# A decoder layer on one core: one norm chain in self-attention, value weights one step sooner, another VectorE order at the end of cross-attention

## The reference, cut to what matters

```python
x = x + attn(_layernorm(x))      # self-attention
x = x + xattn(_layernorm(x), ctx, ctx, mask)   # cross-attention to 128 keys, 16 heads of 64
x = x + ffn(_layernorm(x))       # shared expert and 32 routed experts, top 1

def attn(residual):              # _layernorm once more, with gain g and bias b
    x = _layernorm(residual, g, b)
    q = heads of x (4 of 128);  k = w_fc.reshape(-1, 128);  v = w_proj.T.reshape(-1, 128)
    return residual + square(relu(q k^T)) v
```

## Time and profile before

| | us |
|---|---|
| median of 3 runs | 2863.79 (2860.95 to 2864.35) |
| the profiled execution, its own time | 2861.03 |
| its span in the trace | 2859.4 |
| TensorE busy in the span | 2772.2 (97%) |
| VectorE busy | 1804.1 (63%) |
| ScalarE busy | 1592.0 (56%) |
| GpSimd busy | 1015.1 (36%) |
| granted TensorE clock, mean | 0.996 of full speed |

### The profile page before, as it was taken

One profiled execution on the slowest core, in us unless ns is written; L12 is line 12 of the kernel. 1 busy time (PEld: TensorE's weight loads), 2 busy tenths in 40 slices (PEclk: granted clock), 3 DMA queues, 4 the chain that ended last, 5 costly groups with the idle time before them and its releaser, 6 DMA issues.

```text
span 2859.4 us, 46307 instructions
## 1 busy us (share of the span) xinstructions
PE 2772.2 (97%) x13287; PEld 2284.7 (80%) x13289; DVE 1804.1 (63%) x2744; ACT 1592.0 (56%) x2744; POOL 1015.1 (36%) x692
## 2 busy tenths in 40 slices
PE   7999999999989999999899999999999999999998
PEld 5888888888778887788778888887788888888886
DVE  6566666666776665667563433435885855676776
ACT  6888888887665554566431111112574744565665
POOL 6888888887522221222200000000232322232332
PEclk9999999999999999999999999999999999999999
DMA  1000000002221102110221111112986964786884
GB/s 63 26 27 11 26 26 26 17 24 70 75 67 45 44 29 59 34 37 28 96 89 59 61 66 60 59 66 87 344 314 216 355 214 146 271 296 228 291 289 175
DMA packets 190791, 322.70 MB, mean 113 GB/s; under 512 B 23528, under 2 KB 49128, under 8 KB 190720
## 3 DMA queue, kind: packets, MB, share of 16 engines
q1 hardware_dynamic: 179440, 296.61, 30.2%
q0 software_dynamic: 11280, 25.20, 2.6%
HBM read 286.86 MB, written 46.66 MB: 117 GB/s over the span
## 4 chain that ended last, share of the span: by engine, by line
PE 86%; DVE 6%; ACT 4%; issue 2%; POOL 1%; ACTq 0%; DMA 0%; DVEq 0%; POOLq 0%
PE d_pG L1977 9%; PE d_pU L1977 8%; PE a_pS L47 4%; PE a_pS L49 4%; PE a_pS L48 4%; PE a_pO L47 4%; PE a_pO L49 4%; PE a_pO L48 4%; PE d_pD L47 3%; PE d_pD L49 3%; PE d_pD L48 3%; PE c_pD L47 2%; PE c_pD L49 2%; PE c_pG L47 2%; PE c_pD L48 2%
## 5 line engine op out<-in xcount | busy, mean ns | idle before, releaser
L157 POOL TENSOR_TENSOR a_pL<-a_p,a_pH 128x1024 fp32r<-128x1024 f32 x256 | 617.8, 2418 | 163.7 <-DVE a_p L348 161.7
L1215 DVE TENSOR_TENSOR e_wL<-e_raw,e_wH 128x1024 fp32r<-128x1024 f32 x384 | 450.3, 1217 | 36.1 <-PE d_pU L1977 24.4
L348 DVE TENSOR_TENSOR a_p<-a_r,a_pS 128x1024 f32<-128x1024 f32 x256 | 312.2, 1220 | 243.4 <-ACT a_r L165 236.2
L1210 ACT CAST e_wH<-e_raw 128x1024 fp32r<-128x1024 f32 x384 | 384.5, 1053 | 86.3 <-PE d_pD L49 59.3
L670 POOL TENSOR_TENSOR b_S<-b_S,b_ri 128x512 f32<-128x512 f32 x128 | 133.2, 1041 | 501.0 <-DVE b_ri L831 501.0
L165 ACT ACTIVATE a_r<-a_pS 128x1024 f32<-128x1024 f32 x256 | 261.8, 1023 | 80.3 <-PE a_pS L49 78.6
L165 ACT ACTIVATE a_pH<-a_r 128x1024 fp32r<-128x1024 f32 x256 | 271.9, 1062 | 9.1
L687 ACT ACTIVATE b_S<-b_S,b_nm 128x128 f32<-128x128 f32 x512 | 198.8, 393 | 35.3 <-DVE b_nm L826 34.7
L1459 POOL DMA_INDIRECT out<-d_og,c_iw x46 | 86.5, 1880 | 359.2 <-DVE d_og L1851 359.2
L47 PE MATMUL a_pS<-a_qH,a_kH 128*128 (+1 forms) x512 | 205.0, 400 | 1.3 <-DVE a_p L348 1.2
L47 PE MATMUL a_pO<-a_pH,a_vH 128*128 128x512 f32 x512 | 199.8, 390 | 1.5 <-POOL a_pL L157 1.5
(11 more groups left out here) (308 smaller groups left out, 7251.2 us busy)
## 6 DMA issues: line engine op xcount, KB each, us to landing
e_raw<-in_L_ffn_routed_gate_w SPq DMA_DIRECT2D x256, 256.0 KB, 4.5
e_raw<-in_L_ffn_routed_up_w SPq DMA_DIRECT2D x256, 256.0 KB, 5.7
e_raw<-in_L_ffn_routed_down_w SPq DMA_DIRECT2D x128, 512.0 KB, 6.8
a_xb<-in_x SPq DMA_DIRECT2D x8, 1024.0 KB, 5.5
x<-a_base SPq DMA_DIRECT2D x32, 256.0 KB, 2.3
b_xr<-x SPq DMA_DIRECT2D x32, 256.0 KB, 3.2
x<-b_xr SPq DMA_DIRECT2D x32, 256.0 KB, 3.0
c_xb<-x SPq DMA_DIRECT2D x32, 256.0 KB, 2.9
```

The costliest lines, as they stand in the source:

```text
L157: nc.gpsimd.tensor_tensor(pL[:, j % RING, :, :], p[:, j % 2, :, :], pH[:, j % RING, :, :].bitcast(F32), ALU.subtract).then_inc(s["low"], 1)
L348: v.tensor_tensor(p[:, j % 2, :, :], r[:, j % 2, :, :], pS[j % 2][:, :, :], ALU.mult).then_inc(s["p"], 1)
L1210: copy(self.wH[n][:, :, :], self.raw[n][:, :, :]).then_inc(self.s["high"], 1)
L1215: unit.tensor_tensor(self.wL[n][:, :, :], self.raw[n][:, :, :], self.wH[n][:, :, :].bitcast(self.F32), self.sub).then_inc(self.s["low"], 1)
```

## The change

In the self-attention the two scales are made side by side: r1 from v + e and r1 r2 from v (1 + e) + e^2, as two halves of 128 x 2 x 4 tiles, in 5 parts with 14 links in place of 9 with 29. At the start the first head's 128 columns of the four tiles are normalised and handed to TensorE by a semaphore of their own, and the other 384 columns after the first copy a_qH. Value weights (1, n) are copied in the steps 12, 14, 16 and 18 (their subtraction follows one step later). In the last two steps of cross-attention VectorE takes the subtractions of pieces 0 and 1 in step 7, after the maximum, and t_low there ahead of the mask; pieces 2 and 3 go into `ending`. A semaphore that nothing waits for (warm) is dropped.

```diff
-    LINKS = 29
+    LINKS = 14
...
         def normalize(G, t):
             if t == 0:
                 act.wait_ge(s["own"], LINKS * (G + 1))
-                if not (isinstance(G, int) and G == 0):
-                    act.wait_ge(s["xt"], NH * G)
+                act.wait_ge(s["xt"], NH * G)
             scaled(qn[:, t, :], G, t, scale, shift).then_inc(s["normed"], 1)
+
+        def normalize_first(t, columns, count):
+            scaled(qn[:, t, columns], 0, t, scale, shift, columns).then_inc(s[count], 1)
...
+        act.wait_ge(s["own"], LINKS)
         for t in range(GT):
-            normalize(0, t)
+            normalize_first(t, slice(0, P), "first")
         q_high(0, 0)
+        for t in range(GT):
+            normalize_first(t, slice(P, C), "normed")
...
+            for w in (w2, w2_ps):
+                v.tensor_scalar(w[:, 0, :], mv_ps[:, :, 1], EPS, None, ALU.add)
+                m = v.tensor_scalar(w[:, 1, :], mv_ps[:, :, 1], 1.0 + EPS, EPS * EPS, ALU.mult, ALU.add)
+            link(m)
...
+        def newton(link):
+            link(v.scalar_tensor_tensor(out=t2_ps, in0=y2_ps, scalar=-0.5, in1=y2[:, :, :], op0=ALU.mult, op1=ALU.mult))
+            link(v.tensor_tensor(t2_ps, t2_ps, w2[:, :, :], ALU.mult))
+            both(link, lambda out: v.scalar_tensor_tensor(out=out, in0=t2_ps, scalar=1.5, in1=y2[:, :, :], op0=ALU.add, op1=ALU.mult))
+
+        def row_scales(link):
+            v.tensor_scalar(up[:, :], y2_ps[:, 0, :], 1.0, None, ALU.add)
+            v.tensor_scalar(scale[:, :], y2_ps[:, 1, :], 1.0, None, ALU.mult)
+            for out, y in ((off, y2[:, 0, :]), (shift, y2[:, 1, :])):
+                m = v.scalar_tensor_tensor(out=out[:, :], in0=mv_ps[:, :, 0], scalar=-1.0, in1=y, op0=ALU.mult, op1=ALU.mult)
+            link(m)
...
-        PARTS = 9
+        PARTS = 5
...
             if h == 0:
-                pe.wait_ge(s["normed"], GT * G + GT)
+                first = isinstance(G, int) and G == 0
+                pe.wait_ge(s["first"], GT) if first else pe.wait_ge(s["normed"], GT * G + GT)
+            if isinstance(G, int) and G == 0 and h == 1:
+                pe.wait_ge(s["normed"], GT)
...
-    W_HIGH_AT = {1: (0, 0), 4: (0, 1), 7: (0, 2), 10: (0, 3), 13: (1, 0), 15: (1, 1), 17: (1, 2), 19: (1, 3),
+    W_HIGH_AT = {1: (0, 0), 4: (0, 1), 7: (0, 2), 10: (0, 3), 12: (1, 0), 14: (1, 1), 16: (1, 2), 18: (1, 3),
...
-                soon = b > pb and j == 0 or j == NPAIR - 2 and not last
+                soon = b > pb and j == 0 or j == NPAIR - 2 or j == NPAIR - 1 and last
...
                 maximum(n, j)
-                if j != NPAIR - 2 and not (last and j == NPAIR - 1):
+                if last and j == NPAIR - 1:
+                    aside(j)
+                elif j != NPAIR - 2:
                     q_low(n + 2, (j + 2) % NPAIR)
...
-                if j in (1, 6, 7) and last:
+                if j == 1 and last:
                     aside(j)
...
             else:
-                w_low(2 * (j - 6))
-                w_low(2 * (j - 6) + 1)
+                w_low(0)
+                w_low(1)
...
             x_low(0, 0)
+            w_low(2)
             norm(0, 3)
+            w_low(3)
             out_stats(g, 0)
```

More of the change, by code:

```diff
@@ L79, in self_attention @@
     st = at(small, "st", [P, GT, 6], F32)
-    var, var1, var2, r1, r2, up, off, scale, shift, gT, bT = (at(small + 96 + 32 * i, n, [P, GT], F32) for i, n in
-                                                              enumerate("v v1 v2 r1 r2 up off scale shift gT bT".split()))
+    w2, y2 = (at(small + 96 + 32 * i, n, [P, 2, GT], F32) for i, n in enumerate(("w2", "y2")))
+    up, off, scale, shift, gT, bT = (at(small + 160 + 32 * i, n, [P, GT], F32) for i, n in
+                                     enumerate("up off scale shift gT bT".split()))
     names = ExitStack()
@@ L168, in piece, with scaled @@
             return a.rearrange("p (a c) -> p a c", a=KC)
-        def scaled(out, G, t, scale, shift):
-            return nc.scalar.activation(out, xb[:, bass.ds(G % 2, 1), t, :].rearrange("p o c -> p (o c)"), ACT.Identity,
-                                        bias=shift[:, t:t + 1], scale=scale[:, t:t + 1])
+        def scaled(out, G, t, scale, shift, columns=slice(0, C)):
+            rows = xb[:, bass.ds(G % 2, 1), t, columns].rearrange("p o c -> p (o c)")
+            return nc.scalar.activation(out, rows, ACT.Identity, bias=shift[:, t:t + 1], scale=scale[:, t:t + 1])
         def normalize(G, t):
@@ L249, in aggregate @@
             link(m)
-            v.tensor_scalar(var[:, :], mv_ps[:, :, 1], 1.0, None, ALU.mult)
-            v.tensor_scalar(var1[:, :], mv_ps[:, :, 1], EPS, None, ALU.add)
-            link(v.tensor_scalar(var_ps, mv_ps[:, :, 1], EPS, None, ALU.add))
-        def both(link, ps, own, op):
-            op(ps)
-            link(op(own))
-        def seed(link, y_ps, y):
-            link(v.tensor_single_scalar(tmp_ps.bitcast(I32), var_ps.bitcast(I32), 1, op=ALU.logical_shift_right))
-            both(link, y_ps, y[:, :], lambda out: v.tensor_scalar(out.bitcast(I32), tmp_ps.bitcast(I32), -1.0, float(0x5F3759DF),
-                                                                  ALU.mult, ALU.add))
@@ L264, in newton @@
-        def newton(link, y_ps, y, var):
-            link(v.scalar_tensor_tensor(out=tmp_ps, in0=y_ps, scalar=-0.5, in1=y[:, :], op0=ALU.mult, op1=ALU.mult))
-            link(v.tensor_tensor(tmp_ps, tmp_ps, var[:, :], ALU.mult))
-            both(link, y_ps, y[:, :], lambda out: v.scalar_tensor_tensor(out=out, in0=tmp_ps, scalar=1.5, in1=y[:, :], op0=ALU.add, op1=ALU.mult))
-        def second_variance(link):
-            link(v.tensor_tensor(tmp_ps, r1_ps, r1[:, :], ALU.mult))
-            link(v.tensor_tensor(tmp_ps, tmp_ps, var[:, :], ALU.mult))
-            both(link, var_ps, var2[:, :], lambda out: v.tensor_scalar(out, tmp_ps, EPS, None, ALU.add))
@@ new lines, in aggregate, with both, seed @@
+            link(m)
+        def both(link, op):
+            op(y2_ps)
+            link(op(y2[:, :, :]))
+        def seed(link):
+            link(v.tensor_single_scalar(t2_ps.bitcast(I32), w2_ps.bitcast(I32), 1, op=ALU.logical_shift_right))
+            both(link, lambda out: v.tensor_scalar(out.bitcast(I32), t2_ps.bitcast(I32), -1.0, float(0x5F3759DF), ALU.mult, ALU.add))
+        def newton(link):
+            link(v.scalar_tensor_tensor(out=t2_ps, in0=y2_ps, scalar=-0.5, in1=y2[:, :, :], op0=ALU.mult, op1=ALU.mult))
+            link(v.tensor_tensor(t2_ps, t2_ps, w2[:, :, :], ALU.mult))
+            both(link, lambda out: v.scalar_tensor_tensor(out=out, in0=t2_ps, scalar=1.5, in1=y2[:, :, :], op0=ALU.add, op1=ALU.mult))
@@ L283, in scales @@
                 aggregate(G, link)
-                seed(link, r1_ps, r1)
+                seed(link)
             elif part <= 3:
-                newton(link, r1_ps, r1, var1)
-            elif part == 4:
-                second_variance(link)
-                seed(link, r2_ps, r2)
-            elif part <= 7:
-                newton(link, r2_ps, r2, var2)
-            else:
-                residual_scales(link)
-        PARTS = 9
+                newton(link)
+            else:
+                row_scales(link)
+        PARTS = 5
         def q_affine(G, h):
@@ L1310, in feed_forward @@
          ("const g_in rH rL x_in0 x_in1 r_in0 r_in1 normed xt xH xL gate up sig gated h hH hL logit_ps lt logit top own score xs xs_out"
[L1311 removed]
+          " down sum out0 out1 w_in0 w_in1 w_in2 w_in3 w_high w_low").split()}
     rs = {n: ctx.enter_context(nc.semaphore("r_" + n)) for n in
@@ L1521, in _ @@
         nc.scalar.activation(rH, rw[:, :, :], ACT.Copy).then_inc(s["rH"], 1)
-        nc.scalar.activation(first_silu[:, :], ident[0:1, 0:1], ACT.Sigmoid).then_inc(s["warm"], 1)
+        nc.scalar.activation(first_silu[:, :], ident[0:1, 0:1], ACT.Sigmoid)
         w_high(KC)
```

10 lines of the change are left out of this document (2 added, 8 removed).

## The result

The changed kernel takes 2839.52 us, the median of six runs (2837.18 to 2841.95). The kernel before, run beside it, takes 2863.81 us (six runs, 2860.80 to 2865.39). The ratio is 0.9917, with a 95% interval of 0.9904 to 0.9930: faster by 24.3 us. The forecast was 2843.0, with a range of 2837 to 2852.

What follows compares the result with a forecast made beforehand. TensorE, busy 97% of the span, was taken as the bound, so only its stands could be won. 3.4 + 5.7 + 10.8 = 19.9 us off 2861.0, adjusted towards the median, gave 2843 us, range 2837 to 2852.

Steps and rivals of the forecast that it cites:

- The start: Kernel start: shorter VectorE chain and split normalisation bring TensorE's first transposes 3.4 us earlier, bounds 1.9 and 3.9.
- The value weights: TensorE's two waits on b_wL: earlier copies gain 5.7 us, including 1.2 us for low clock; bounds 1.5 and 7.1.
- So 1.1 us of the second wait stays: Value weights: the last moved subtraction ends near 744.0 us, TensorE ready at 742.9, leaving 1.1 us of wait.
- My hand schedule: Value weights: hand-worked VectorE times after the move, a_p of steps 16, 18, 19 ending near 726.6, 735.9, 740.1 us.
- The rule weighed there: Value weights: VectorE instructions with two SBUF inputs and GpSimd ones reading SBUF exclude each other, whichever starts first.
- 15.1 us, the sum by that reading: Total gain if four moved subtractions each held GpSimd up 1.2 us and all 4.8 us reached TensorE.
- GpSimd keeps the value weights late: Rival, chance 0.12: moved subtractions find GpSimd busy, value weights gain only 1.5 us; sum 15.7, time 2847 us.
- The end: End of cross-attention: VectorE's new order removes both long waits on b_tL, last products 10.8 us earlier; bounds 8.5 and 11.5.
- the end gives the moved subtractions back: Rival, chance 0.09: `ending` loses 2.3 us to subtractions and as much to a late reload; gain 15.3, time 2848 us.
- the change doesn't do what it says: Rival, chance 0.03: other TensorE waits fill both long gaps, only the start's gain is won; 2860 us, no change.
- The sum: Whole kernel: gains of 3.4 at the start, 5.7 at the value weights and 10.8 at the end total 19.9 us.
- From the profiled execution's 2861.0 us: Step from gain to time: 2861.0 becomes 2841.1 us; adding the median's 2.8 us offset gives 2843.9, taken as 2843.

Runs made afterwards that it cites:

- after_again: The changed kernel itself, run again on another chip; median 2839.40 us, ratio 0.9920 to the kernel before.
- start_only: Kernel before with the self-attention part alone (one chain of 14 links, first 128 columns first); median 2858.86 us, ratio 0.9984.
- values_only: Kernel before with the value weights' copies in steps 12, 14, 16 and 18 alone; median 2854.20 us, ratio 0.9967.
- values_first_pair: Kernel before with value pieces (1,0) and (1,1) alone copied in steps 12 and 14; median 2859.21 us, ratio 0.9987.
- chain_only: Kernel before with the single chain alone, the four tiles normalised whole; median 2860.31 us, ratio 0.9990.
- end_only: Kernel before with VectorE's new order in cross-attention's last two steps and behind it alone; median 2851.83 us, ratio 0.9962.
- split_only: Kernel before with the first 128 columns normalised ahead of the rest, old chains kept; median 2862.43 us, ratio 0.9995.
- end_second_pair: Kernel before with only the subtractions of pieces 2 and 3 moved into `ending`; median 2858.43 us, ratio 0.9982.
- warm_gap: Changed kernel with eight identity transposes on TensorE after the key transposes; median 2838.15 us, ratio 0.9914 to the kernel before.
- values_filled: Kernel before with TensorE's two waits on b_wL filled with 20 and 14 identity transposes; median 2860.64 us, ratio 0.9991.
- warm_both: Changed kernel with 40 identity transposes ahead of the key transposes and 12 behind; median 2837.47 us, ratio 0.9912 to the kernel before.

## Why the prediction was right, and where it was off

**The start**: predicted 3.4 us, with bounds of 1.9 and 3.9. Measured 3.4 at the first scores, and 3.5 to 3.7 by b_k1H in two traces of three. The steps hold one by one: chain until 12.8 us (forecast 12.8), ScalarE late with a_kH (14.0 forecast, 13.95), pieces 1.64 us for 1.5, transposes at 15.53 for 15.5, the rest 2.49 us for 2.5. What was not in the sum is the clock of the first scores: at half clock in the first trace after, it took 1.3 us of the gain (27.8 against 26.4 us at the stand behind a_vL), and at full clock in after_again and start_only nothing.

**The value weights**: predicted 5.7 us, bounds 1.5 and 7.1; measured 6.8 and 6.9. This is the mis-sized term. The step that failed is "So 1.1 us of the second wait stays": none stayed. My hand schedule had the subtraction of (1, 3) end near 744.0 us with TensorE ready at 742.9. The trace to hold against it is that of values_only, whose start is before's (b_k1H at 696.4 us for 696.2). TensorE was there at 742.93, as forecast, but the subtraction ended at 742.66: a_p of the steps 16, 18 and 19 ended at 726.4, 735.1 and 739.1 us where I had 726.6, 735.9 and 740.1, so VectorE was earlier by 0.2, 0.8, 1.0 and at last 1.3 us. In the trace after all of this lies 2.4 us earlier (740.25 and 740.53), as its b_k1H does. The margin is 0.3 us in both. That subtractions beside GpSimd stretch was right in kind: 2.98 and 2.98 us, 1.78 at (1, 1).

The rule weighed there (the Trainium skill, SBUF — State Buffer, "Who interferes with whom") shows here in one direction: the instruction that starts second is blocked for what is left of the other. The subtraction at 728.59 us took 2.98 us, which is the rest of GpSimd's low part (until 730.49 us) and 1.1 of its own. The other direction, 1.2 us lost on GpSimd four times over, didn't occur: all eight low parts from 710 to 744 us take 2.39 to 2.41 us, and none starts while one of the subtractions runs, so no run here shows that direction. So 15.1 us, the sum by that reading, was too low. The rival *GpSimd keeps the value weights late* fell.

**The end**: predicted 10.8 us, bounds 8.5 and 11.5; measured 10.7 to 10.8 in all traces with this part. Remaining waits forecast at 1.9, 0.7 and 0.8 us are 1.95 (1404.53), 0.78 and 0.82 (1412.38); the fourth, 1.84 us for the last b_aL (1415.44), was there before as well. The moved subtractions cost nothing, as forecast: VectorE's idle 1.33 and 2.40 us in `ending` shrank to 0 and 1.53. The rival *the end gives the moved subtractions back* fell with it, and so did "the change doesn't do what it says".

**The sum**: 19.9 us against 19.1 and 21.6 in two traces. **The time**: 2843.0 against 2839.5. The medians differ by 24.3 us, 4.4 more than the sum. After_again, whose profiled execution lies at its median, has 1.7 of them in its ledger: 0.3 at the start, 1.2 at the value weights, 1.1 behind c_pG, less 0.1 at the end and 0.8 in cross-attention. The other 2.7 are in "From the profiled execution's 2861.0 us": I carried the offset of 2.8 us between it and the median over to the changed kernel, as if the change couldn't touch it. Two of three executions of before take about 3 us more than the profiled one. By the traces named above that is 1.8 us of half clock behind the second wait for the value weights, which goes with the wait, and about 1.0 us in cross-attention, which both traces of the changed kernel have too. Counted from such an execution, the value weights give 6.9 + 1.8 = 8.7 us, cross-attention 0.2, and with 3.7, 10.7 and 1.1 the ledger comes to 24.4 us, for 24.0 to 24.3 measured. This is an estimate, since no trace shows such an execution of before. By it the value weights are above their bound of 7.1: I had 1.2 us for the clock, behind the first wait alone. For values_only it makes 6.8 + 1.8 = 8.6 us against 9.9 by the medians, whose interval reaches from 6.0 to 12.9.

**Luck.** That 2839.5 lies in the range of 2837 to 2852 is owed in part to how the range was counted. The gain of 24.3 us (20.0 to 27.5 by the interval) is larger than all high ends together (22.5). From the median of 2863.8 us these give 2841.3, and the measured time is below that. It is inside because the lower end was counted from the profiled execution's 2861 and then widened by 1.5 us.

## What to carry to other kernels

When the value of an edit is a stand of TensorE, count the wait in the rows, and add the half clock that may follow it as a separate term with its own chance: a profile shows one draw of it. Where profiled execution and median differ by more than the spread of the runs around their mode, look for such a stand before forecasting from the profile. A wait that can't be shortened can be filled with throw-away transposes, which here recovered the clock's share alone. And when two traces of different kernels are subtracted, compare the clock window by window first, also where the change does nothing: values_first_pair's 3.0 us would else be taken for the worth of its pair.

## What the runs showed of the hardware that was not expected

The same stand, in the same kernel text, is followed by half clock in some executions and not in others. Behind the second wait for b_wL, 2.3 to 2.4 us, the clock was 1.00 in before, start_only and chain_only and 0.91 in end_only, split_only, end_second_pair and values_first_pair; of these the first three take 66.0 to 67.2 us from the first values product to b_pQ, where before takes 64.2. Behind the stand for a_vL (2.29 to 2.33 us in every kernel) it fell in five traces (after, warm_gap, split_only, end_second_pair and values_filled) and stayed up in the other eight. Behind the stand of 2.32 us for b_S it fell in seven and stayed up in six.

A window of the profile can read a clock of 1.00 where there is no record of the clock. In after:

```profile
17.60:22.00 4.40, 4.40 (x16) 3.59 (x15) 0.69 (x1) 3.07 (x6) 0.00 (x0) 1.00 0.00 0
```

The stretch reads 1.00 with sixteen passes, although the passes from 19.2 to 21.7 us lie 0.43 us apart; after_again, at a spacing of 0.23, fits 22 into the same window. The first record of the clock in after's trace starts at 21.6 us, at full clock, which is where the spacing changes. In chain_only it starts at 13.1 us, and there the half clock of 18 to 20 us is recorded (0.52). Near the start of a trace the spacing is what to go by.

Identity transposes count for the clock. The sixteen key transposes behind forty of the same kind in warm_both took 1.73 us, in warm_gap, without those forty, 3.04 (9.53 us on). In warm_gap the clock's first record, at full clock, starts at 12.3 us, when only transposes had run; eight more (0.91 us) and a stand of 1.61 us later it was still up, and the next four loads took 0.42 us instead of 0.71. That it was the eight that kept it up is not shown, since no trace has that stand without them. The Trainium skill, TensorE: Matmul & The Clock Gate, "Part 4: PE-mode transpose", says that a transpose doesn't bring the full clock. Here the measurement decides against the page.
